# Products with the values behind three and five scores in turn, and every second score maximum taken from its two banks one after the other

## The reference

```python
scores = jnp.einsum('bhqd,bhkd->bhqk', Q, K) / np.sqrt(HD).astype(np.float32)
w = jax.nn.softmax(scores, axis=-1)
attn = jnp.einsum('bhqk,bhkd->bhqd', w, V)
```

## Time and profile before

| | |
|---|---|
| median of 3 runs | 1074.57 us (1072.9 to 1076.34) |
| the profiled execution | 1073.3 us, span 1071.5 us |
| PE busy | 1031.2 us, 96% of the span |
| DVE busy | 793.7 us, 74% |
| ACT busy | 650.4 us, 61% |
| POOL busy | 265.6 us, 25% |
| granted TensorE clock, mean | 0.998 |
| first and last score (L427) | 62.7 and 802.9 us |
| last maximum (L931) | 766.9 us |

### The profile page before, as it was taken

How to read it: one execution, slowest core, us unless ns; L and a number is a source line. 1 busy time by engine, 2 the same in 40 slices (tenths; PEclk the granted TensorE clock), 3 DMA queues, 4 the chain that set the end, 5 groups by cost and what they waited for, 6 DMA issues and landing times.

```text
span 1071.5 us, 15045 instructions
## 1 busy us (share of the span) xinstructions
PE 1031.2 (96%) x5736; PEld 552.5 (52%) x5736; DVE 793.7 (74%) x911; ACT 650.4 (61%) x1224; POOL 265.6 (25%) x227
## 2 busy tenths in 40 slices
PE   8999999999999999999999999999999999999996
PEld 3643344433443433443344443333347888888885
DVE  5889978899779799779978889999812475662545
ACT  2368877778678788678766668888773331222221
POOL 2651030042335423146200042843100000000002
PEclk9999999999999999999999999999999999999999
DMA  6174417243242512354140436431127810504011
GB/s 212 66 204 115 105 38 209 52 97 76 53 114 72 99 59 57 76 111 102 35 77 12 115 113 155 119 111 50 67 94 168 188 40 1 118 15 65 1 39 42
DMA packets 64428, 94.83 MB, mean 89 GB/s; under 512 B 37536, under 2 KB 37920, under 8 KB 62272
## 3 DMA queue, kind: packets, MB, share of 16 engines
q1 hardware_dynamic: 63776, 93.10, 34.4%
q10 hardware_dynamic: 576, 0.72, 0.2%
HBM read 53.95 MB, written 27.00 MB: 76 GB/s over the span
## 4 chain that ended last, share of the span: by engine, by line
PE 80%; ACT 14%; DVE 2%; issue 1%; DMA 1%; SPq 0%; POOL 0%; POOLq 0%
PE PV L446 24%; PE PS L427 21%; PE PSA L516 14%; ACT Bn L732 11%; PE PS L533 5%; PE PS L348 4%; PE PSA L409 2%; PE PS L472 2%; PE PSA L472 2%; ACT Bn L740 2%; PE PV L533 1%; PE PSA L348 1%; PE PS L390 1%; DVE nmx L931 1%; DMA wr<-A 1%
## 5 line engine op out<-in xcount | busy, mean ns | idle before, releaser
L931 DVE TENSOR_REDUCE nmx<-PSA 128x1 f32<-128x1024 f32 x512 | 599.8, 1217 | 87.7 <-PE PSA L409 87.6
L732 ACT ACTIVATE Bn<-PS 128x512 f32<-128x512 f32 x1024 | 530.0, 605 | 144.3 <-PE PS L427 143.3
L427 PE MATMUL PS<-Qt,Kt 50*128 50x512 f32 x1024 | 373.5, 446 | 25.2 <-ACT Bn L732 12.5
L409 PE MATMUL PSA<-Kt,Qt 48*128 48x512 f32 x1024 | 394.7, 464 | 2.0 <-DVE nmx L931 1.0
L427 PEld LDWEIGHTS PS<-Qt,Kt 50*128 50x128 f32 x1024 | 167.4, 184 | 321.4 <-ACT Bn L732 298.8
L446 PE MATMUL PV<-Bn 128*32 128x512 f32 x2048 | 272.8, 605 | 0.0
L409 PEld LDWEIGHTS PSA<-Kt,Qt 48*128 48x128 f32 x1024 | 166.7, 184 | 30.1 <-DVE nmx L931 13.7
L516 PE MATMUL PSA<-x1Th,wr 128*128 128x512 f32 x344 | 135.1, 393 | 1.1 <-DMA wr<-A 0.6
L516 PE MATMUL PSA<-x1Tl,wr 128*128 128x512 f32 x344 | 134.9, 392 | 0.0
L1017 DVE SCALAR_TENSOR_TENSOR sg<-PSA,us,sg 128x512 f32<-128x512 f32 x43 | 32.1, 748 | 104.2 <-ACT sg L767 104.2
L767 ACT ACTIVATE sg<-PSA,gs 128x512 f32<-128x512 f32 x43 | 29.5, 690 | 128.6 <-PE PSA L516 128.6
(11 more groups left out here) (163 smaller groups left out, 828.5 us busy)
## 6 DMA issues: line engine op xcount, KB each, us to landing
Qt<-pscr SPq DMA_DIRECT2D x90, 128.0 KB, 4.8
A<-in_wf SPq DMA_DIRECT2D x11, 768.0 KB, 6.2
wr<-A SPq DMA_DIRECT2D x33, 256.0 KB, 3.9
pscr<-A SPq DMA_DIRECT2D x16, 512.0 KB, 3.7
vscr<-Bn SPq DMA_DIRECT2D x32, 256.0 KB, 2.0
Kt<-pscr SPq DMA_DIRECT2D x90, 64.0 KB, 2.5
A<-A SPq DMA_DIRECT2D x16, 256.0 KB, 3.7
Bn<-vscr SPq DMA_DIRECT2D x8, 512.0 KB
```

The source lines that it names most:

```text
L409: op = e.matmul(PSA[:, 2 * s + h, :], Qt[n % 3][p:p + NC_, g % 2, 128 * qt:128 * qt + 128], Kt[n % 3][p:p + NC_, 512 * h:512 * h + 512], s ...
L427: e.matmul(PS2[:, c % 3, :], Kt[n % 3][rows, 128 * kt:128 * kt + 128], Qt[n % 3][rows, g % 2, 512 * qh:512 * qh + 512], start=True, stop=T ...
L732: e.activation(Pb[c % NP_], PS2[:, c % 3, :], ACT.Exp, scale=0.25).then_inc(*act_exp.next(c))
L931: e.tensor_reduce(nmx[:, hh % 2, c0:c0 + 1], slot_pair(s), AX.XY, ALU.max, negate=True).then_inc(*dve_max[s].next(k))
```

## The change

In the loop over units 0 to 243 the product with the values of unit `u - 1` stands behind the third score of unit `u` where `u` is even, and behind the fourth where it is odd. So between two products there are three and five scores in turn, where there were four. The last 12 units keep their order.

Of every step whose head is below 2, DVE reduces the two banks one after the other, each 512 columns, into two columns; each has its own wait and its own increment, PE increments for both halves, and the next first half in that slot waits for the first reduction only. `turn_max` first joins the eight extra columns with a minimum (the maxima are stored negated).

```diff
--- before.py
+++ after.py
@@ -94,7 +94,7 @@
         st = sb("st", [128, 4, 6])
         mv = sb("mv", [128, 4, 2])
         ve = sb("ve", [128, 2, 4])
-        nmx = sb("nmx", [128, 2, 16])
+        nmx = sb("nmx", [128, 2, 24])
         msp = sb("msp", [128, 32], F32R)
         mrow = sb("mrow", [128, 2, 32])
         dn = sb("dn", [128, 64])
@@ -282,6 +282,10 @@
         def slot_of(k):
             return (k + (k >= before_flag)) % 2
 
+        def by_halves(k):
+
+            return stream[k][2] < 2
+
         def slot_pair(s):
             return PSA[:, 2 * s:2 * s + 2, :]
 
@@ -324,6 +328,7 @@
         def tensor(e):
             w = Once(e)
             bank_free, slot_free = [None] * 4, [None] * 2
+            first_half_free = [None] * 2
 
             def clear(point):
                 if point:
@@ -398,8 +403,8 @@
                 k, h = divmod(j, 2)
                 n, qt, g = stream[k]
                 s = slot_of(k)
+                clear(first_half_free[s] if h == 0 and first_half_free[s] else slot_free[s])
                 if h == 0:
-                    clear(slot_free[s])
                     if n == 0:
                         for point in first_rows[qt // 4]:
                             w.wait_ge(*point)
@@ -408,9 +413,12 @@
                 p = 64 * (g // 2)
                 op = e.matmul(PSA[:, 2 * s + h, :], Qt[n % 3][p:p + NC_, g % 2, 128 * qt:128 * qt + 128],
                               Kt[n % 3][p:p + NC_, 512 * h:512 * h + 512], start=True, stop=True)
+                if h == 0 and by_halves(k):
+                    op.then_inc(*pe_max.next((k, 0)))
                 if h == 1:
                     op.then_inc(*pe_max.next(k))
                     slot_free[s] = dve_max[s].at(k)
+                    first_half_free[s] = dve_max[s].at((k, 0)) if by_halves(k) else None
 
             def scores(u, g):
                 n, v = divmod(u, 16)
@@ -479,7 +487,7 @@
                 w.wait_ge(*dve_flag.at("max"))
                 w.wait_ge(*dve_const.at())
                 e.matmul(slot_pair(s)[0:1, 0, 0:1], lowb[:, :], ones[:, :], start=True, stop=True).then_inc(*pe_flag.next())
-                slot_free[s] = dve_flag.at("flag")
+                slot_free[s], first_half_free[s] = dve_flag.at("flag"), None
 
             def turn_rows(x, tb, pair):
                 s = ffn_slots(x)["turn", 2 * tb + pair]
@@ -647,8 +655,8 @@
                 for g in range(4):
                     scores(u, g)
                     advance(1)
-                if u >= 1:
-                    weigh(u - 1)
+                    if u >= 1 and g == (2, 3)[u % 2]:
+                        weigh(u - 1)
                 if at_u in project_at:
                     for h, i in enumerate(free_banks(u)):
                         project_half(project_at[at_u], h, i, (0, 1, 2, 3))
@@ -924,19 +932,29 @@
                     return
                 s, hh = slot_of(k), k // 16
                 g, qt = stream[k][2], stream[k][1]
-                w.wait_ge(*pe_max.at(k))
+                c0 = 4 * g + qt % 4
                 if hh >= 2:
                     w.wait_ge(*dve_ms.at(("low", hh - 2)))
-                c0 = 4 * g + qt % 4
-                e.tensor_reduce(nmx[:, hh % 2, c0:c0 + 1], slot_pair(s), AX.XY, ALU.max, negate=True).then_inc(
-                    *dve_max[s].next(k))
+                if by_halves(k):
+                    w.wait_ge(*pe_max.at((k, 0)))
+                    e.tensor_reduce(nmx[:, hh % 2, 16 + c0:17 + c0], slot_pair(s)[:, 0, :], AX.X, ALU.max, negate=True).then_inc(
+                        *dve_max[s].next((k, 0)))
+                    w.wait_ge(*pe_max.at(k))
+                    e.tensor_reduce(nmx[:, hh % 2, c0:c0 + 1], slot_pair(s)[:, 1, :], AX.X, ALU.max, negate=True).then_inc(
+                        *dve_max[s].next(k))
+                else:
+                    w.wait_ge(*pe_max.at(k))
+                    e.tensor_reduce(nmx[:, hh % 2, c0:c0 + 1], slot_pair(s), AX.XY, ALU.max, negate=True).then_inc(
+                        *dve_max[s].next(k))
                 if k % 16 == 15:
                     turn_max(hh)
 
             def turn_max(hh):
-                top = nmx[:, hh % 2, :]
+                top, rest = nmx[:, hh % 2, 0:16], nmx[:, hh % 2, 16:24]
                 for k in (16 * hh + 14, 16 * hh + 15):
                     w.wait_ge(*dve_max[slot_of(k)].at(k))
+                e.tensor_tensor(top[:, 0:8], top[:, 0:8], rest, ALU.min).then_inc(*dve_ms.next(("join", hh)))
+                w.wait_ge(*dve_ms.at(("join", hh)))
                 if hh >= 1:
                     w.wait_ge(*dve_ms.at(("turn", hh - 1)))
                 e.tensor_copy(msp[:, 0:16], top).then_inc(*dve_ms.next(("high", hh)))
```

## The result

The changed kernel takes 1067.26 us (median of 4 runs, 1066.94 to 1067.64), against 1074.43 of the kernel before in the same comparison: ratio 0.9928, 95% interval 0.991 to 0.9946. The forecast was 1072 with 1063 to 1083; its own narrower band, 1068 to 1076, is missed by 0.7.

The account below looks back on a forecast made before the run. The prediction took a circle of PE and ACT, not DVE, as the bound. Its terms, -24.8 + 6.3 + 12.3 + 3.6 + 0.5 = -2.1 us, gave 1072 us, range 1063 to 1083.

Parts of the forecast that it names:

- turning costs nothing: Rival, chance 0.17: O3's half (odd unit's fourth score) does not end last behind a turning; 6.3 us more gained, 1066.
- circle of PE and ACT: Scores, exponentials and products waiting on each other bound the loop: 2.60 us per unit; new pair 4.97 instead of 5.20.
- The term of 24.8 us: Gain in ordinary pairs of units: 0.23 us less per pair in 108 or so pairs, -24.8 us.
- Halves at 0.60: DVE's 512-column reductions take a slot of 0.60 us each, leaving DVE idle 0.30 of a 4.97 us pair.
- The copy: ACT's copy of PV, now between an even unit's last exponential and the next: 0.41 more, 30 times, +12.3 us.
- The turning: Turning sixteen maxima after units 8n + 3 makes DVE late, the next pair's product 0.33 later: 19 times, +6.3 us.
- The casts: Six ACT casts in even units, formerly free, now cost some 0.6 us each: +3.6 us.
- Behind a block: In the pair behind a block the even unit's third score waits for ACT's eviction: no gain, 0.
- ahead of the loop: Ahead of the loop and around the flag, extra 4 x 0.07 and one join of 0.21: +0.5 us.
- The split is void: Rival, chance 0.07: DVE's first half is late like an undivided reduction; mild form gains nothing, 1075 to 1078 us.
- DVE becomes the bound: Rival, chance 0.15: dearer half reductions, from 0.69 us each, make DVE limit the loop; slower, 1082 to 1084 us.
- A cold start behind E2: Rival, chance 0.13: product behind an even unit's third score starts after 0.43, not 0.32; +11.9 us, so 1084.

Follow-up runs that it names:

- the order alone: Kernel before with only the products with the values moved, every maximum still one whole reduction of 1024 columns: 1112.62 us, ratio 1.0357.
- the halves alone: Changed kernel with every product behind the fourth score again, as before, keeping the divided reductions: 1074.26 us, ratio 1.0003 to the kernel before.
- The early copy: Changed kernel with ACT's copy of PV behind the third exponential of an even unit instead of the fourth: 1056.55 us, ratio 0.9836 to the kernel before.
- three joins: Changed kernel with the join of the maxima done three times, each waiting for the one before: 1078.13 us, ratio 1.0036 to the kernel before.
- every step in halves: Changed kernel with every step's maximum taken bank by bank, the join over 16 columns: 1069.54 us, ratio 0.9932 to the kernel before.

## Why the prediction was right, point by point

The bound, the direction and the range held. The size did not fully: the forecast was a gain that no measurement could tell from none, and the kernel is 0.7% faster, under the band of 1068 to 1076 that the forecast's own chance of 0.48 stood for. The time is close to the 1066 of the rival "turning costs nothing", but that rival's reason is not what happened.

- **The circle of PE and ACT** as the bound, and its new length of 4.97 us: seen as 4.98. The term of 24.8 us stands; the order alone and the halves alone show that it needs both.
- **Halves at 0.60.** A half starts, and what follows it, 0.59 to 0.60 apart, as the row that read SBUF had it. DVE's idle time in an ordinary pair is 0.24, forecast 0.30.
- **The copy.** Its interval is longer by 0.49 and was by 0.09 before: 0.40 net against a forecast of 0.41. The early copy shows it directly.
- **The turning** was the term that was mis-sized. A single one costs 0.28, forecast 0.33. But only 14 groups pay it, not 19: in the five others without a block a cast in the even unit (3.61) makes PE wait 0.5, and DVE has caught up by then (three joins, 0.42 longer, cost 0.41 in the 14 and only 0.16 in the five). 14 x 0.28 = 3.9 us instead of 6.3.
- **The casts** cost 0.51 each, forecast 0.6, and there are seven of them (I had left out the one of unit 2): 3.6 us, as forecast, but by luck, since two errors cancel.
- **Behind a block** nothing was to be gained. By the terms above (three ordinary pairs and one copy) a group with a block should take some 0.3 us less. Eight of the eleven take 26.50 to 26.61 us where they took 26.69 to 26.88, one 28.18 for 28.31, and the two with a cast 27.01 and 27.12 for 26.76 and 26.91. So without a cast it is 0.2 on average.
- The loop from the first product to that of unit 240 takes 689.9 us against 694.4: 4.5 us less, forecast 2.6 with these terms. The turning by itself gives 2.4, and the groups with a block take part of that back. 0.4 was gained ahead of the loop, where I had put a loss; that says little, since the same stretch of the same program ended at 64.52 in the halves alone and at 66.22 here. A last 0.8 lies behind the product of unit 240, 0.7 of it behind the last product: the chain of before has a transfer of weights of 8.8 us there, that of the changed kernel has none. Why it fell out was not tried.
- **The rivals.** "The split is void" and "DVE becomes the bound" are excluded by the order alone and by every step in halves. A cold start behind E2 is not there (0.32). "Turning costs nothing" is excluded by the 3.38 behind a turning and by the join done three times.

## What to carry to other kernels

Where two in-order engines wait for each other in a circle, lay one period out by hand from the rows before and after the change; small operations beside the circle cost their whole time or nothing, by which side of a wait they stand on, and here moving one of them (10.7 us) was worth more than the change itself (7.2 us). A change of order may need a finer grain on a third engine before it pays; the order alone cost 39 us. Measure both alone before dropping either.

## What the runs showed of the hardware that I had not expected

- A DVE operation on 8 columns lasted up to 1.22 us instead of 0.17 while a POOL operation with two inputs ran, and ended with it. Over seven kernels I found 23 drawn-out rows of joins and casts behind the maxima, and each ends within 0.04 us of the end of such a POOL operation. In the changed kernel the join never met one (0.167 to 0.170 us, 32 times); its time holds only as long as that is so.
- A wait of 1.08 us on PE was followed by 6.8 us at half clock, and not each time: behind the same join of 1.20 us the clock stayed at its upper level, 2.4 GHz, in two other groups of that run. Over the two kernels, six of ten waits of 0.86 to 1.08 us were followed by a fall. So one blocked operation of 1.2 us cost between 1.0 and 4.0 us in a group of eight units. What decides whether the clock falls stays open.
